# The output projection of a tile pair as seven block products instead of eight, in an attention kernel on one core

## What is computed

```
q, k, v = heads(x @ Wq + bq), heads(x @ Wk + bk), heads(x @ Wv + bv)
scores = einsum('bhqd,bhkd->bhqk', q, k) / sqrt(32)
attn = softmax(where(adj[:, None] == 0, -inf, scores))
out = einsum('bhqk,bhkd->bhqd', attn, v)          # heads side by side: 512 columns
y = x + out @ Wo + bo
result = (y - mean(y)) / sqrt(var(y) + 1e-5)      # per row
```

## Time and profile before

| | |
|---|---|
| median of 3 runs | 822.01 us (821.75 to 822.07) |
| profiled execution | 821.39 us |
| its span, first to last instruction | 819.5 us |
| mean granted TensorE clock | 0.999 of 2.4 GHz |
| TensorE matmul busy | 812.0 us, 99% |
| VectorE, GpSimd, ScalarE busy | 544.9, 512.6, 238.2 us |

### The profile page before, as it was taken

The page is one execution under the profiler, slowest core; times in us unless marked ns, Lnnn a source line. Parts: engine busy times, 40 slices in busy tenths (PEclk is TensorE's granted clock), DMA queues, the critical chain, the costliest instruction groups (busy, mean ns, idle before and its releaser), DMA issues.

```text
span 819.5 us, 25422 instructions
## 1 busy us (share of the span) xinstructions
PE 812.0 (99%) x11286; PEld 665.1 (81%) x11286; DVE 544.9 (66%) x691; ACT 238.2 (29%) x315; POOL 512.6 (63%) x407
## 2 busy tenths in 40 slices
PE   9999999999999999999999999999999999999997
PEld 7788888888888888888888888888888888888886
DVE  5667667766567666676665776656766567766795
ACT  6532233221332222332223322133322233223223
POOL 1386667656675565856658566576665767657682
PEclk9999999999999999999999999999999999999999
DMA  9224424253342433424334243352424434234342
GB/s 321 90 79 122 120 81 135 84 143 95 88 143 72 149 92 92 139 70 142 105 91 134 71 144 95 82 154 82 128 88 106 136 82 131 84 108 118 105 105 104
DMA packets 50173, 92.37 MB, mean 113 GB/s; under 512 B 11280, under 2 KB 13328, under 8 KB 47888
## 3 DMA queue, kind: packets, MB, share of 16 engines
q1 hardware_dynamic: 47568, 87.08, 36.2%
q10 hardware_dynamic: 2496, 3.67, 1.6%
HBM read 40.37 MB, written 16.78 MB: 70 GB/s over the span
## 4 chain that ended last, share of the span: by engine, by line
PE 98%; DVE 1%; POOL 0%; ACT 0%; issue 0%; POOLq 0%; DVEq 0%
PE ring L289 23%; PE ring L291 21%; PE ring L290 21%; PE ring L386 7%; PE ring L387 7%; PE ring L390 7%; PE psum_s L357 6%; PE ring L375 6%; PE ring L407 1%; PE ring L309 0%; POOL soft L912 0%; PE ring L313 0%; PE ring L317 0%; DVE soft L717 0%; DVE top L724 0%; ACT soft L568 0%
## 5 line engine op out<-in xcount | busy, mean ns | idle before, releaser
L912 POOL TENSOR_TENSOR soft<-soft,top 128x1024 f32<-128x1024 f32 x62 | 125.2, 2020 | 77.5 <-DVE top L724 77.5
L171 POOL TENSOR_TENSOR soft<-soft,inverse 128x1024 f32<-128x1024 f32 x62 | 118.9, 1918 | 24.9 <-DVE inverse L731 22.2
L563 ACT ACTIVATE kt<-ring,bk 128x512 f32<-128x512 f32 x64 | 43.6, 681 | 258.7 <-PE ring L291 258.6
L889 POOL TENSOR_TENSOR x_lo<-x_raw,x_hi 128x512 fp32r<-128x512 f32 x56 | 72.0, 1286 | 61.1 <-ACT x_hi L548 61.1
L289 PE MATMUL ring<-wv_hi,x_hi 128*128 128x512 f32 x256 | 103.5, 404 | 0.0
L289 PE MATMUL ring<-x_hi,wk_hi 128*128 128x512 f32 x256 | 103.1, 403 | 0.0
L728 DVE TENSOR_REDUCE total<-soft 128x16 f32<-128x1024 f32 x62 | 75.6, 1219 | 41.0 <-ACT soft L568 41.0
L291 PE MATMUL ring<-wv_hi,x_lo 128*128 128x512 f32 x256 | 100.1, 391 | 0.0
L291 PE MATMUL ring<-x_hi,wk_lo 128*128 128x512 f32 x256 | 99.9, 390 | 0.0
L290 PE MATMUL ring<-x_lo,wk_hi 128*128 128x512 f32 x256 | 99.7, 390 | 0.0
L290 PE MATMUL ring<-wv_lo,x_hi 128*128 128x512 f32 x256 | 99.6, 389 | 0.0
(11 more groups left out here) (81 smaller groups left out, 1362.3 us busy)
## 6 DMA issues: line engine op xcount, KB each, us to landing
pt<-soft SPq DMA_DIRECT2D x464, 64.0 KB, 2.0
x_raw<-in_xt SPq DMA_DIRECT2D x15, 1024.0 KB, 6.8
row<-in_x SPq DMA_DIRECT2D x60, 256.0 KB, 2.7
out_rows<-row SPq DMA_DIRECT2D x60, 256.0 KB, 2.6
adj<-in_adj SPq DMA_DIRECT2D x16, 128.0 KB, 2.9
pt<-soft ACTq DMA_DIRECT2D x32, 64.0 KB, 2.2
kt<-in_wk SPq DMA_DIRECT2D x4, 256.0 KB, 5.1
row<-in_wv SPq DMA_DIRECT2D x1, 1024.0 KB, 8.4
```

What stands on the lines that cost most here:

```text
L171: ops.tensor_tensor(soft_of(c), soft_of(c), on_keys(inverse[:, c % 2, :]), ALU.mult).then_inc(normed, 1)
L889: nc.gpsimd.tensor_tensor(x_lo[:, buf, :, rows], x_raw[:, :, rows], x_hi[:, buf, :, rows].bitcast(F32), ALU.subtract).then_inc(x_lo_done, 1)
L912: nc.gpsimd.tensor_tensor(soft_of(c), soft_of(c), on_keys(top[:, c % 2, :]), ALU.subtract).then_inc(centred, 1)
```

## The change

For pairs 0 to 26 the two output projections (each tile's 128 x 512 rows times Wo, 512 x 512) become one product of a 2 x 2 block matrix (two tiles by two halves of the 512 features) with a 2 x 2 block matrix (Wo in quarters), by a scheme with seven block products instead of eight. Each block product has 2 chunks of 128 features x 3 parts = 6 matmuls of 256 columns. Four of the factors are sums of row blocks (`s_raw`, split into `s_hi` and `s_lo`), and four are sums of weight blocks (`t_hi`, `t_lo`), made once at the start. The last pairs keep `project_out`.

To make the sums, ScalarE now first copies the mixed rows as they are from PSUM (`ot_raw`, in the place of one `pt` buffer, of which two are left), then rounds that copy; VectorE adds and subtracts blocks of it (`add_rows`), with the `_lo` parts between (`split_blocks`); ScalarE rounds the sums (`split_sums`), and GpSimd makes their `_lo` part. VectorE adds the products to the residual rows in parts (`add_part`). Of the scheme's products four are issued between Q of b and V of b, one after the next scores and two after the next K; TensorE's Q of b moves behind V of a. The rows' normalisation moves from VectorE to ScalarE (`norm_by_act`, with one more small GpSimd operation, `make_shift`), and rows are finished, stored and loaded about a turn later. The bias is kept once per tile, not four times, and mask reads it in two halves. At the start GpSimd makes the weight sums and their `_lo` part.

The core of the diff, in the order TensorE, ScalarE, VectorE, GpSimd, SP (constants, buffers, semaphore counts and the tail's counterparts are left out):

```diff
+            def product(out, left_hi, left_lo, right_hi, right_lo, adds=False):
+                for kc in range(2):
+                    nc.tensor.matmul(out, left_hi[:, kc, :], right_hi[:, kc, :], start=kc == 0 and not adds, stop=False,
+                                     skip_group_check=adds)
+                    nc.tensor.matmul(out, left_hi[:, kc, :], right_lo[:, kc, :], start=False, stop=False,
+                                     skip_group_check=adds)
+                for kc in range(2):
+                    last = nc.tensor.matmul(out, left_lo[:, kc, :], right_hi[:, kc, :], start=False, stop=kc == 1,
+                                            skip_group_check=adds)
+                return last
...
+            def first_products(m):
+                pe.wait_ge(masked, 4 * (m + 2))
+                pe.wait_ge(ot_hi_done, m + 1)
+                pe.wait_ge(ot_lo_first, m + 1)
+                pe.wait_ge(ot_lo_done, m + 1)
...
+                product(first_bank()[:, 0:HALF], *rows_block(0, 1), *weights_block(1, 0))
+                product(first_bank()[:, HALF:D], *rows_block(1, 1), *weights_sum(4)).then_inc(y_part, 1)
+                product(ring[:, 2, 0:HALF], *rows_block(0, 0), *weights_block(0, 0)).then_inc(y_part, 1)
+                pe.wait_ge(s_hi_done, m + 1)
+                pe.wait_ge(s_lo_done, m + 1)
+                product(ring[:, 3, 0:HALF], *rows_sum(1), *weights_sum(1)).then_inc(y_part, 1)
+            def middle_product(m):
+                pe.wait_ge(row_part, PARTS * m + P1)
+                product(ring[:, 2, 0:HALF], *rows_sum(2), *weights_sum(2), adds=True).then_inc(y_part, 1)
+            def last_products(m):
+                pe.wait_ge(row_part, PARTS * m + P6)
+                product(ring[:, 2, 0:HALF], *rows_sum(3), *weights_sum(3), adds=True).then_inc(y_part, 1)
+                product(ring[:, 3, 0:HALF], *rows_sum(4), *weights_block(1, 1), adds=True).then_inc(y_part, 1)
...
                 score(a)
                 score(b)
+                if p >= 2:
+                    middle_product(p - 2)
                 pe.wait_ge(v_done, a - 1)
                 project_k(a + 4)
+                if p >= 2:
+                    last_products(p - 2)
                 pe.wait_ge(v_done, a)
                 project_q(a + 4)
                 pe.wait_ge(k_done, a + 5)
                 project_k(b + 4)
-                pe.wait_ge(q_done, a + 5)
-                project_q(b + 4)
-                wait_for(pe, row_added, a - 2)
+                wait_for(pe, row_part, PARTS * (p - 1))
                 mix(a - 2)
                 mix(b - 2)
                 pe.wait_ge(k_done, b + 5)
                 project_v(a)
+                pe.wait_ge(q_done, a + 5)
+                project_q(b + 4)
+                first_products(p - 1)
                 pe.wait_ge(q_done, b + 5)
                 project_v(b)
-                pe.wait_ge(ot_lo_done, p)
-                project_out(a - 2)
-                project_out(b - 2)
...
+            def read_pair(m):
+                act.wait_ge(mixed, 2 * m + 2)
+                nc.scalar.copy(ot_raw().rearrange("p t c (g q) -> p (t c) g q", g=2),
+                               mixed_rows(m, slice(0, 2))).then_inc(ot_raw_done, 1)
+                act.wait_ge(ot_raw_done, m + 1)
+                wait_for(act, y_part, PARTS * (m - 1) + P1)
+                nc.scalar.copy(ot_hi[:, :, :, :], ot_raw()).then_inc(ot_hi_done, 1)
+            def split_sums(m):
+                act.wait_ge(s_raw_done, 4 * (m + 1))
+                nc.scalar.copy(s_hi[:, :, :, :], s_raws(m)).then_inc(s_hi_done, 1)
...
                 read_k(b + GT)
-                read_q(b + GT)
                 if p == 0:
+                    read_q(b + GT)
                     place(a)
-                if p >= 1:
-                    read_ot(p - 1)
+                else:
+                    read_pair(p - 1)
+                    split_sums(p - 1)
+                    read_q(b + GT)
                 for c in (a, b):
+                    if p >= 2:
+                        norm_by_act(c - 4)
...
+                for b in range(2):
+                    nc.vector.tensor_tensor(
+                        soft_of(c)[:, b].rearrange("p (r c) k -> p r c k", r=HC), psum_s[:, :, c % 2, b],
+                        bias[:, c // GT % 2, c % GT, b].unsqueeze(1).unsqueeze(1).to_broadcast([P, HC, KC, SQ]),
+                        ALU.add).then_inc(masked, 1)
...
+            def split_blocks(m):
+                dve.wait_ge(ot_hi_done, m + 1)
+                nc.vector.tensor_tensor(ot_lo[:, 0], ot_raw()[:, 0], ot_hi[:, 0].bitcast(F32),
+                                        ALU.subtract).then_inc(ot_lo_first, 1)
+                nc.vector.tensor_tensor(ot_lo[:, 1, 2:4, :], raw_block(1, 1), ot_hi[:, 1, 2:4, :].bitcast(F32),
+                                        ALU.subtract).then_inc(ot_lo_done, 1)
+            def add_rows(m):
+                dve.wait_ge(ot_raw_done, m + 1)
+                done = 4 * m
+                nc.vector.tensor_tensor(s_raw(m, 2), raw_block(0, 0), raw_block(1, 0), ALU.subtract).then_inc(s_raw_done, 1)
+                nc.vector.tensor_tensor(s_raw(m, 0), raw_block(1, 0), raw_block(1, 1), ALU.add).then_inc(s_raw_done, 1)
+                split_blocks(m)
+                dve.wait_ge(s_raw_done, done + 2)
+                nc.vector.tensor_tensor(s_raw(m, 1), s_raw(m, 0), raw_block(0, 0), ALU.subtract).then_inc(s_raw_done, 1)
+                dve.wait_ge(s_raw_done, done + 3)
+                nc.vector.tensor_tensor(s_raw(m, 3), raw_block(0, 1), s_raw(m, 1), ALU.subtract).then_inc(s_raw_done, 1)
...
+                mask(a)
                 if p >= 2:
-                    add_row(a - 3)
-                mask(a)
+                    add_sixth(p - 2)
                 mask(b)
+                sum_up(a)
                 if p >= 2:
-                    norm_row(dve, nc.vector, a - 3)
-                sum_up(a)
+                    add_last(p - 2)
                 sum_up(b)
                 turn(a)
+                if p >= 2:
+                    row_sums(a - 4)
+                if p >= 1:
+                    add_rows(p - 1)
                 turn(b)
+                read_v(a)
                 if p >= 1:
-                    split_ot(p - 1)
-                read_v(a)
+                    add_first(p - 1)
+                if p >= 2:
+                    row_sums(b - 4)
+                if p >= 1:
+                    add_middle(p - 1)
                 read_v(b)
-                if p >= 1:
-                    add_row(a - 2)
-                    norm_row(dve, nc.vector, a - 2)
...
+            def split_sums(m):
+                pool.wait_ge(s_hi_done, m + 1)
+                nc.gpsimd.tensor_tensor(s_lo[:, :, :, :], s_raws(m),
+                                        s_hi[:, :, :, :].bitcast(F32), ALU.subtract).then_inc(s_lo_done, 1)
...
+            add_weights()
+            split_weight_sums()
             pool.wait_ge(vo_b_in, DMA * 2)
...
                 normalise(pool, nc.gpsimd, b)
-                add_bo(a)
+                if p >= 1:
+                    add_bo(a - 2)
+                    add_bo(b - 2)
+                if p >= 2:
+                    make_shift(a - 4)
+                if p >= 1:
+                    split_sums(p - 1)
+                if p >= 2:
+                    make_shift(b - 4)
...
-                if p >= 2:
-                    store(a - 3)
-                place(a)
+                place(a)
+                place(b)
+                if p >= 2:
+                    store(a - 4)
+                    store(b - 4)
+                load_row(a)
                 load_row(b)
-                place(b)
-                if p >= 1:
-                    store(a - 2)
-                load_row(b + 1)
```

More of the change, by code:

```diff
@@ L178, in by_chunk, with ot_raw, raw_block, s_raws @@
             return ot[:, tiles, :, :].rearrange("p t c (g q) -> p (t c) g q", g=2)
+        def ot_raw():
+            return pt[:, 1].rearrange("p q h k -> p (q h k)").rearrange("p (t c n) -> p t c n", t=2, c=KC)
+        def raw_block(i, j):
+            return ot_raw()[:, i, 2 * j:2 * j + 2, :]
+        def s_raws(m):
+            return v[:, 2 * m % 4:2 * m % 4 + 2, :].rearrange("p t (n c q) -> p (t n) c q", n=2, c=2)
+        def s_raw(m, n):
+            return s_raws(m)[:, n]
+        def w_raw_block(i, j):
+            return w_raw[3][:, 2 * i:2 * i + 2, j * HALF:(j + 1) * HALF]
+        def t_raw(n):
+            return pt[:, n // 2, n % 2, :, :].rearrange("p h k -> p (h k)").rearrange("p (c n) -> p c n", c=2)
+        def quarter(m, i, j):
+            return row[:, (2 * m + i) % 4, j * HALF:(j + 1) * HALF]
+        def first_bank():
+            return psum_s[:, 0].rearrange("p t b c k -> p (t b c k)")
         def ot_count(c):
@@ L205, in place @@
                 sp.wait_ge(turned, c + 1)
-                wait_for(sp, mixed, c - 3)
+                wait_for(sp, mixed, pt_users(c))
+                if c < 2:
```

(53 more changed lines are left out.)

135 lines of the change are left out of this document (85 added, 50 removed).

## The result

The changed kernel takes 873.3 us (median of four runs, 871.2 to 874.7) against 821.9 us before: a ratio of 1.062, with a 95% interval of 1.060 to 1.065. It is slower by 51 us. The time lies just inside the stated range (813 to 874); it is that of the second rival (873, chance 0.16), not the 849 of the likeliest case. The profiled execution has a span of 872.8 us, against 819.5.

A forecast was written before the change was run, and what follows sets the result against it. TensorE, busy 99% of the span, was taken as the bound: 821.4 - 10.8 (matmuls) + 36 (waits before the fourth product) + 2 (start) = 848.6, so 849 us with the median's 0.6; range 813 to 874.

The forecast's parts named there:

- second rival: GpSimd's whole add_bo holds VectorE's two-SBUF-input subtractions: some 2.3 us a pair, 873 us in all, chance 0.16.
- likeliest case: Only the first part of a GpSimd operation holds VectorE: 1.4 us a pair, 849 us, own range 840 to 860, chance 0.42.
- matmul term: Output projections: 24 matmuls of 512 columns become 42 of 256, saving 0.40 us a pair, 10.8 us over 27 pairs.
- places in the turn: Positions from the scores' start: mixing at 12.07 us, first block product 19.07, the fourth issued 21.23, V of b 21.95.
- the chain: ScalarE copies, VectorE subtractions, ScalarE rounding, GpSimd's 2.4 us ahead of the fourth product: ready at 21.2, needed by 21.23.
- step that failed: VectorE's six two-SBUF-input subtractions beside GpSimd: 0.84 us lost at each of two meetings, 1.3 us on the chain.
- The start: First turns: first mask 0.4 us late, and V waiting 1.5 us for read_k(7) in turn 1; 2 us together.
- edits costed at nothing: Other VectorE, ScalarE, GpSimd and SP edits: priced at no cost, with 0.4 us of cover for add_sixth before last_products.

The follow-up runs named there:

- e1_no_bias: Changed kernel with GpSimd's add_bo on 1 column instead of 512 for the 54 block-scheme tiles: 823.0 us, ratio 1.0006 to the kernel before.
- e5_long_bo: Changed kernel with GpSimd adding the bias to both rows in one 1024-column operation instead of two of 512: 873.5 us.
- e10_one_input: Changed kernel with each block-scheme add_bo replaced by a GpSimd multiplication by 1 with one SBUF input: 835.7 us in one run.
- e3_psum: Changed kernel with each of VectorE's six subtractions taking one input from PSUM instead of SBUF: 821.4 us, ratio 0.9991 to the kernel before.
- e8_place: e3_psum with ScalarE issuing a turned tile's transfers ahead of the x split in the first two turns: 817.6 us, ratio 0.9938.
- e9_start: e8_place with weight-block sums moved from GpSimd to VectorE, ScalarE rounding them in turn 0, and VectorE making two `_lo` parts: 816.6 us, ratio 0.9928.
- e4_v_earlier: Changed kernel with V of b before the fourth issued product, and VectorE reading V before add_middle: 823.7 us, ratio 1.0021 to the kernel before.
- e2_bo_early: Changed kernel with GpSimd's two add_bo before normalise(b) instead of behind it: 827.6 us, ratio 1.0072 to the kernel before.

## Why the prediction came out as it did

**The matmul term** was right in its rows: 0.120 us for each product's matmul. Its size was smaller than I wrote: 24.91 us a turn without waits, not 24.76, so 0.25 us saved per pair and not 0.40. In a turn of e1_no_bias the seven products take 5.24 us (0.82 behind the scores, 1.43 behind K, 2.99 for the four ahead of V of b) where the two output projections took 5.53 (425.36 - 419.83), and the six other projections 16.74 where they took 16.70. Some 0.11 of the missing 0.15 us are at the fourth product issued, whose wait ends just in time: it starts about 0.05 us late, and its second matmul 0.19 behind its first, not 0.12. The rest is a few hundredths where a projection follows products. Behind the scores the second matmul comes 0.10 us late (0.22, not 0.12), but so it did before (0.34, not 0.23).

**The places in the turn** were right to a few hundredths: the products 7.02 us behind the mixing, the first copy 1.52 us behind it, GpSimd's subtraction of 1024 columns 2.37 us where I took 2.4. Without the holding the chain is in time, as priced.

**The step that failed** is "only the first part of a GpSimd operation holds VectorE". I had one meeting, in which VectorE got in after 0.9 of 3.65 us, and took it as the rule; e5_long_bo and e10_one_input show that beside float32 operations the hold follows the GpSimd operation's length. The two subtractions lose 1.10 us each, not 0.84: 1.8 us on the chain instead of 1.3. The Trainium skill, "SBUF — State Buffer", section "Who interferes with whom", had both halves of this: the later one is blocked for the whole instruction (stated there for VectorE's 2-port modes), and an operation with at most one SBUF input does not contend. The 2.64 us of e5_long_bo and the 0.42 us of e3_psum agree with it; the bias operation, which lets VectorE in after a quarter of its length, does not. So the one meeting that I generalised from was the exception. Why it is one stays open; the repeated reading is ruled out, as shown above.

**The second rival** has the right mechanism; its right total is luck. It charged 2.2 us per pair plus 0.1 for the chain, where 1.77 was lost, some 14 us too much over 26 pairs. Against that it counted the matmul gain some 4 us too high and the start 10 us too low, and it had neither the late products at the end (2.2 us) nor the turn with half the clock (1.8 us).

**The start** was priced at 2 us and cost 12.0 by turn 3. The wait for K ahead of V in turn 1 was foreseen, at 1.5 us; it is 1.84. The rest is two turns' waits before the fourth product (1.60 and 1.94 us), held splits at the start, two stretches at half the clock, and what I had not seen: ScalarE's transfers for tile 3 stand behind a split that waits for V of b. I moved V of b to the end of the turn in my head and did not go through what ScalarE had queued behind it. e8_place shows that it mattered.

**The edits costed at nothing** (add_sixth ahead of last_products, SP, ScalarE's new order) were covered: with the chain in time, TensorE waits nowhere in the regular turns.

## What to carry to other kernels

When a change gives VectorE operations with both inputs in SBUF, look at what GpSimd does in the same microseconds, and add the rest of GpSimd's operation to each (measured here for float32 operations of 512 and 1024 columns); a copy of one input that lies in PSUM anyhow costs the same and avoids it. A product split into more and narrower matmuls must be counted in instructions as well as in columns: here an eighth fewer columns left 0.40 of 5.44 us by the instructions, and the borders took 0.15 of those. When a step moves to the end of a loop's turn, follow every queue that waits for it, the transfers issued there as well.

## What the runs showed of the hardware that was not expected

TensorE's granted clock, full in the kernel before until its matmuls are over, fell three times in the middle of the profiled run of the change, each time for about 3 us: at 64, 105 and 187 us. The third is in the turn that lasted 28.48 us, against 26.66 for its neighbours. One-microsecond stretches (length, busy time of the engines and counts, then granted clock, DMA share, GB/s):

```profile
183.00:184.00 1.00, 1.00 (x11) 1.00 (x10) 1.00 (x2) 1.00 (x2) 0.28 (x1) 1.00 0.09 23
...
185.00:186.00 1.00, 0.00 (x0) 0.00 (x0) 0.94 (x2) 0.43 (x1) 1.00 (x1) 1.00 0.45 109
...
187.00:188.00 1.00, 1.00 (x6) 0.90 (x6) 0.20 (x1) 0.45 (x1) 0.90 (x3) 0.50 0.41 94
188.00:189.00 1.00, 1.00 (x4) 0.81 (x3) 0.22 (x1) 0.37 (x1) 0.76 (x1) 0.50 0.47 119
```

What TensorE had waited for ahead of the three falls, and one wait that no fall followed (at 92.22):

```profile
63.38 0.50 PE L343 MATMUL ring<-wv_hi,x_hi 128*128 128x512 f32 x1 [1.84 <-ACT kt L674]
92.22 1.48 PE L431 MATMUL ring<-pt,v 64*32 64x64 f32 x128 [1.92 <-DVE row L916]
104.68 0.36 PE L451 MATMUL ring<-t_hi,s_hi 128*128 128x256 f32 x1 [1.94 <-POOL s_lo L1119]
186.46 0.39 PE L451 MATMUL ring<-t_hi,s_hi 128*128 128x256 f32 x1 [1.84 <-POOL s_lo L1119]
```

After the wait of 1.84 us before the fourth product the clock is at 0.50, 1.2 GHz, from about 187 to 190, and the matmuls of that stretch last 0.63 us instead of 0.40; the turn is 1.8 us longer than its neighbours. The other two falls lie in turns 1 and 2, whose length has other causes too. The remaining 25 waits before the fourth product, 1.60 to 1.63 us each, left the clock alone, but so did the 1.92 us at 92.22: the length of a wait does not by itself decide, and what does stays open. In e1_no_bias, e3_psum and e9_start, where regular turns have no wait, the clock is full until the last products are over (mean 0.998 to 0.999); in e4_v_earlier it fell once, behind a wait of 1.97 us for K in turn 1, and in e2_bo_early twice, behind its first two waits before the fourth product (1.79 and 1.94 us).
